# Two attention layers with a flagged fallback: the opening stage's work dealt anew over three engines, its value products moved earlier, and the first scores placed ahead of the flag's read

## The chip, the cores and the metric

The kernel runs on one core of a Trainium2 chip. The metric is the time of one execution on the device in microseconds (us); the kernel before took 882.53 us in the median of three runs. The engines of a core run their own instruction streams in order and wait for one another through semaphores: TensorE (PE) does matrix products, ScalarE (ACT) activations, VectorE (DVE) and GpSimd (POOL) elementwise work, SyncE (SP) issues the transfers.

## The reference, cut to what matters

```python
x = L0_attn_x                                   # (4, 1024, 128)
xn = _layernorm(x)
s = _L0_attn_ref(xn, ...)                       # its own layernorm of xn, qkv, 16 heads of 8, softmax, output product
g = _silu(_L0_ffn_ref(xn, W_fc, W_proj))        # relu squared FFN, then 5 spiking steps
x = x + s * g
xn = _layernorm(x)
s = _L1_attn_ref(xn, ...)                       # causal attention with position slopes
g = _silu(_L1_ffn_ref(xn, ...))                 # coupling network, 3 cycles
return x + s * g
```

Only what leads up to the first attention is touched: the double normalization of x, the products q, k and v of it, and the transposes of the two FFN weights.

## The kernel before

The 4096 tokens lie in 32 tiles of 128 tokens. The program has four stages on every engine: the prologue (`prologue`), the first attention (`first_attention`), a middle, the second attention. Each stage is a function that gives one part for each engine, and the parts are concatenated, so an engine goes from its prologue to its attention part without a barrier.

The prologue works in eight halves m = 0 to 7 of 512 tokens (four tiles each, the list `M`). For each half there are these steps:

- the normalized tiles `hs` (named xn in the trace), four tensor_scalar instructions in `normalized_by`, L337. VectorE does halves 0, 2 and 4, GpSimd 1, 3, 5, 6 and 7 (`ON_POOL`). They wait for the roots of the variances, which VectorE finds for tiles 0 to 7, 8 to 15 and 16 to 31 in three rounds; each ends in `rooted`.
- `turn(m)`: four transposes on TensorE, L575, into the PSUM bank `tr[m % 2]`; ScalarE copies them to `y`, L411 (`h_kept`).
- q and k: two products of 128x512 on TensorE, L604, into `pq[m % 2]`, which is free when the low parts of half m - 2 are done.
- each of q and k is kept as a high and a low part: ScalarE writes the high part (`high_of`, L414) and the square (`square_of`, L417), VectorE the low part (`low_of`, L490). SyncE stores both to DRAM, from where the stacked operands q_st and k_st are loaded.
- `norms_of(m)`: TensorE sums the squares by head, L585, into the bank `pn`; VectorE takes the maximum of each pair of halves (`peak_of`, L495).

Behind the last half TensorE does the v products of batch 0 (L612), the last norms, the transposes of the two FFN weights (L618, L621; ScalarE copies them, L455), and a transpose of the maxima (L624). VectorE turns them into `flag` in five small steps, L550 to L554: it says whether the scores could overflow. Then it does the last low parts and adds the bias to v (L563).

`row_maxima` follows: TensorE, VectorE and SyncE each read the flag into a register (TENSOR_LOAD, L671 on TensorE) and branch. With this input the flag is 0 and the body is skipped. Only then comes the first score of `first_attention`, L1165.

The first attention has 256 steps t. A step is four score products (L1165) into two of three PSUM slots, two exponentials of 128x1024 on ScalarE (L959), and the products with v (L1182) two steps later. Step t is work of pair t // 2; `side_fills` says at which pair a piece of other work is put between the steps on TensorE (`piece_of`) and on VectorE (`evacuate`). The first of these pieces is fc at pair 5.

Of the kernel before, what the change touches and what calls it, by code (L numbers as in the profile page):

```python
# [32 lines left out]
G = 4  # L33
# [252 lines left out]
def prologue(nc, a, s, x_t, room):  # L286
# [18 lines left out]
    norms, top, peak = piece(1, B), piece(1, 1), piece(1, P)[0:1, :]  # L305
# [19 lines left out]
    link, hs_rdy, hs_pool, tr_ps, ht_in, oned = (sem(x) for x in ("link", "hs_rdy", "hs_pool", "tr_ps", "ht_in", "oned"))  # L325
    qk_ps, kept, squared, lo_rdy, norm_ps, norm_in = (sem(x) for x in ("qk_ps", "kept", "squared", "lo_rdy", "norm_ps", "norm_in"))
    beta_ps, bv_rdy, ffn_ps, ffn_kept, v_ps = (sem(x) for x in ("beta_ps", "bv_rdy", "ffn_ps", "ffn_kept", "v_ps"))
    tail, peak_turned, v_kept = sem("tail"), sem("peak_turned"), sem("v_kept")
    stored = [s[f"stored0{m}"] for m in range(M)]
    room["first_flagged"], room["lows_done"], room["v_kept"] = tail, (lo_rdy, 2 * M), (v_kept, 2)  # L330

    def h_t(m):
        return s["y"][:, HT * m:HT * m + HT, :].rearrange("p t c -> p (t c)")

# [73 lines left out]
    def act_part(act):  # L408
        def h_kept(m):
            act.wait_ge(tr_ps, m + 1)  # L410
            nc.scalar.copy(h_t(m), tr[m % 2]).then_inc(ht_in, 1)  # L411

        def high_of(m, z):
            nc.scalar.activation(parts[m][:, z, 0, :], pq[m % 2][z], ACT.Identity, bias=b_col[:, z:z + 1]).then_inc(kept, 1)  # L414

        def square_of(m, z):
            nc.scalar.activation(square[m % 2][:, z, :], pq[m % 2][z], ACT.Square, bias=b_col[:, z:z + 1]).then_inc(squared, 1)  # L417

# [18 lines left out]
        for m in range(M):  # L437
            if m >= 2:
                act.wait_ge(norm_ps, m - 1)
            if m == M - 1:  # L440
                for z in range(2):
                    act.wait_ge(qk_ps, 2 * m + z + 1)
                    square_of(m, z)
                for z in range(2):
                    high_of(m, z)
                continue
            for z in range(2):
                if z == 1 and 2 <= m + 1 < M:
                    h_kept(m + 1)
                act.wait_ge(qk_ps, 2 * m + z + 1)  # L450
                high_of(m, z)
                square_of(m, z)
        for n, kept_t in enumerate((s["fc_t"], s["proj_t"])):
            act.wait_ge(ffn_ps, n + 1)
            nc.scalar.copy(kept_t[:, :, :], pq[0][n].rearrange("p (n f) -> p n f", n=FC)).then_inc(ffn_kept, 1)  # L455

    def dve_part(dve):
# [22 lines left out]
        def rooted_of(n0, n1):  # L480

            ch.after(nc.vector.tensor_scalar_mul(s["skip_r"][:, n0:n1], rstd[:, 1, n0:n1], GATE_SCALE))
            dve.sem_inc(rooted, 1)

        def normalized(m):
            normalized_by(nc.vector, m).then_inc(hs_rdy, 1)

        def low_of(m, z):
            dve.wait_ge(kept if m == M - 1 else squared, 2 * m + z + 1)
            nc.vector.scalar_tensor_tensor(parts[m][:, z, 1, :], pq[m % 2][z], b_col[:, z:z + 1],  # L490
                                           parts[m][:, z, 0, :].bitcast(F32), ALU.add, ALU.subtract).then_inc(lo_rdy, 1)

# [28 lines left out]
        normalized(2)  # L521
# [4 lines left out]
        for k in range(ROOT_STEPS):  # L526
            root(MIDDLE, NT, k)
            if k in (3, 6):
# [3 lines left out]
        normalized(4)  # L532
# [4 lines left out]
                                ALU.add).then_inc(bv_rdy, 1)  # L537
        ch.after(nc.vector.tensor_tensor(s["rho"][:, :], rstd[:, 1, :], rstd[:, 1, :], ALU.mult))
        nc.vector.tensor_tensor(s["rho"][:, :], s["rho"][:, :], var[:, 0, :], ALU.mult)
        for m in range(2, M - 1):  # L540
            low_of(m, 0)
            low_of(m, 1)
            if m % 2 == 0 and m > 2:
                peak_of(m // 2 - 1)
# [5 lines left out]
        tops.after(nc.vector.tensor_copy(peak, tr[0][0:1, 0:P]))  # L550
# [4 lines left out]
        low_of(M - 1, 0)  # L555
        low_of(M - 1, 1)
        dve.wait_ge(v_zero, 1)
        dve.wait_ge(v_preset, 1)
# [1670 lines left out]
```

## Time and profile before

| | us |
|---|---|
| median of three runs (880.74 to 882.54) | 882.53 |
| the profiled execution | 881.24 |
| its span, from the first to the last instruction | 879.4 |
| start of the first exponential of the attention | 52.62 |

1.84 us of the profiled execution lie outside the span. The page gives the busy time of each engine and, in 40 slices of 22 us, their busy share in tenths; the chain of waits says which instruction released the next; the timeline gives the instructions of an engine in order of time. The granted clock is the share of TensorE's full clock of 2.4 GHz: 1.00, or 0.50 for 1.2 GHz.

### The profile page before, as it was taken

What the parts mean: (1) busy time and instruction counts of PE and PEld (TensorE: products, weight loads), DVE (VectorE), ACT (ScalarE), POOL (GpSimd) and SP (SyncE); (2) the same over time, 40 slices, a digit from 0 to 9 for tenths busy, and PEclk for the clock granted to TensorE, in tenths of its full rate; (3) what the DMA queues carried; (4) which work ended last, traced back from release to release, by engine and by line L of the source; (5) the groups of instructions that cost most, each with busy time, mean ns of one, the idle gap of its engine ahead of it and who ended that gap; (6) DMA issues with size and microseconds to landing.
All of it is one profiled execution on the core that took longest, in us unless ns stands there. A gap on an engine that the chain in (4) does not pass through costs nothing.

```text
span 879.4 us, 21895 instructions
## 1 busy us (share of the span) xinstructions
PE 786.2 (89%) x9238; PEld 302.1 (34%) x9238; DVE 419.0 (48%) x884; ACT 827.2 (94%) x921; POOL 225.6 (26%) x272
## 2 busy tenths in 40 slices
PE   4769999899999999999999999997988988978976
PEld 2322434234343434433343433222332323323322
DVE  7731275464657662677537588996021121131132
ACT  7769999999999999999999996769999999999996
POOL 5401120121212041111303021203234334334333
PEclk9969999999999999999999999997999999999999
DMA  7892020110210300203000016100202113022000
GB/s 189 288 285 49 2 78 2 39 40 2 78 46 6 126 2 14 90 25 111 16 3 25 26 44 207 42 25 1 70 9 89 40 52 89 15 75 90 13 1 25
DMA packets 31947, 53.42 MB, mean 61 GB/s; under 512 B 5481, under 2 KB 16361, under 8 KB 31849
## 3 DMA queue, kind: packets, MB, share of 16 engines
q1 hardware_dynamic: 31848, 52.01, 18.8%
q8 instruction: 74, 1.21, 0.6%
q14 instruction: 25, 0.20, 0.1%
HBM read 31.29 MB, written 20.71 MB: 59 GB/s over the span
## 4 chain that ended last, share of the span: by engine, by line
PE 71%; ACT 18%; DVE 7%; issue 4%; DMA 0%; SPq 0%; DVEq 0%; ACTq 0%
PE c_ps L1182 27%; PE c_ps L1165 13%; ACT c_ring L1874 12%; PE c_ps L112 10%; PE c_ps L2027 8%; PE c_ps L2066 8%; ACT c_ring L959 3%; PE c_ps L1592 1%; DVE early L1537 1%; DVE c_th L463 1%; PE c_ps L1607 1%; ACT xs L1881 1%; PE c_ps L1599 1%; ACT c_ring L1395 1%; DVE y L1540 1%
## 5 line engine op out<-in xcount | busy, mean ns | idle before, releaser
L959 ACT ACTIVATE c_ring<-c_ps 128x1024 f32<-128x1024 f32 x512 | 473.7, 1032 | 7.3 <-PE c_ps L1165 7.0
L1182 PE MATMUL c_ps<-c_ring,vt 128*18 128x256 f32 (+1 forms) x3072 | 272.3, 457 | 0.0
L1874 ACT ACTIVATE c_ring<-c_ps 128x1024 f32<-128x1024 f32 x288 | 267.9, 1070 | 2.4 <-PE c_ps L2027 2.0
L2066 PE MATMUL c_ps<-c_ring,vt 128*18 128x384 f32 (+3 forms) x1672 | 152.7, 467 | 2.4 <-issue 0.9
L1165 PE MATMUL c_ps<-q_st,k_st 32*128 32x512 f32 x1024 | 131.4, 501 | 25.5 <-ACT c_ring L959 20.5
L1899 POOL TENSOR_SCALAR_AFFINE_SELECT c_ring<-c_ring 128x512 f32<-128x512 f32 x128 | 84.3, 677 | 182.3 <-ACT c_ring L1874 182.3
L1182 PEld LDWEIGHTS c_ps<-c_ring,vt 128*18 128x18 f32 x3072 | 64.9, 97 | 143.0 <-issue 103.1
L2027 PE MATMUL c_ps<-q_st,k_st 32*128 32x512 f32 (+3 forms) x768 | 80.0, 418 | 35.1 <-ACT c_ring L1874 31.9
L1165 PEld LDWEIGHTS c_ps<-q_st,k_st 32*128 32x128 f32 x1024 | 50.5, 183 | 142.1 <-ACT c_ring L959 132.8
L980 POOL TENSOR_TENSOR early<-early 128x512 f32<-128x512 f32 x32 | 38.4, 1201 | 176.3 <-DVE early L1103 176.3
L2027 PEld LDWEIGHTS c_ps<-q_st,k_st 32*128 32x128 f32 x768 | 39.8, 186 | 106.3 <-ACT c_ring L1874 94.4
L2066 PEld LDWEIGHTS c_ps<-c_ring,vt 128*18 128x18 f32 x1672 | 35.3, 97 | 58.8 <-issue 43.6
L1933 DVE STREAM_TRANSPOSE ext<-c_ps 128x512 f32<-128x512 f32 x15 | 10.8, 717 | 93.5 <-PE c_ps L2066 93.5
L1103 DVE TENSOR_SCALAR early<-c_ps 128x512 f32<-128x512 f32 x32 | 22.1, 690 | 63.5 <-PE c_ps L112 63.5
L1107 DVE TENSOR_SCALAR y<-c_ps,rho 128x128 f32<-128x128 f32 x32 | 9.0, 344 | 83.4 <-PE c_ps L112 83.4
L966 POOL TENSOR_TENSOR early<-early,y 128x512 f32<-128x512 f32 x7 | 10.6, 1512 | 142.6 <-DVE early L1118 142.6
L1395 ACT ACTIVATE c_ring<-c_ps,cn_b 128x512 f32<-128x512 f32 (+1 forms) x30 | 25.1, 858 | 16.5 <-PE c_ps L1592 9.6
L988 POOL TENSOR_TENSOR c_th<-parts 128x512 bf16<-128x512 f32 x12 | 15.4, 1287 | 82.7 <-DVE parts L1135 82.7
L112 PE MATMUL c_ps<-proj_t,early 128*32 128x128 f32 x1024 | 33.8, 273 | 0.0
L112 PE MATMUL c_ps<-y,fc_t 128*32 128x512 f32 x256 | 33.3, 592 | 0.0
L1954 DVE COPY y<-c_ps 128x512 f32<-128x512 f32 x8 | 5.5, 692 | 58.0 <-PE c_ps L2079 58.0
L112 PEld LDWEIGHTS c_ps<-proj_t,early 128*32 128x32 f32 x1024 | 29.3, 110 | 5.9
(242 smaller groups left out, 774.3 us busy)
## 6 DMA issues: line engine op xcount, KB each, us to landing
q_st<-q_hl SPq DMA_DIRECT2D x48, 256.0 KB
k_st<-k_hl SPq DMA_DIRECT2D x48, 256.0 KB
q_hl<-parts SPq DMA_DIRECT2D x10, 512.0 KB, 4.1
k_hl<-parts SPq DMA_DIRECT2D x10, 512.0 KB, 4.3
q_hl<-c_ring SPq DMA_DIRECT2D x4, 512.0 KB, 3.8
k_hl<-c_ring SPq DMA_DIRECT2D x4, 512.0 KB, 4.6
out_dram<-x SPq DMA_DIRECT2D x7, 256.0 KB, 3.7
x<-in_L_attn_x_dram SPq DMA_DIRECT2D x3, 512.0 KB, 5.8
```

Of the source, the lines that this page charges most:

```text
L112: ins = nc.tensor.matmul(out[c:c + COLUMN, :], weight[:, c:c + COLUMN], rows, start=start, stop=stop, tile_position=(0, c))
L959: nc.scalar.activation(probs[t % RING][:, 2 * pair:2 * pair + 2, :], scores[unit % SLOTS][:, :, :], ACT.Exp).then_inc(expd, 1)
L980: pool.tensor_tensor(hidden[f], hidden[f], hidden[f], ALU.mult).then_inc(hid_rdy, 1)
L988: pool.tensor_tensor(square[hf][:, z, :], high, high, ALU.mult).then_inc(sq_rdy, 1)
L1103: ins = nc.vector.tensor_scalar_max(hidden[hf[1]], side[:, :], 0.0)
L1165: ins = nc.tensor.matmul(scores[(2 * t + i // 2) % SLOTS][:, i % 2, :], k_st[part, g, kt * P:(kt + 1) * P], q_st[part, g, qh * HALF:(qh + ...
L1182: ins = nc.tensor.matmul(o_ps[32 * h:32 * h + 2 * W9, c0:c1], vt[b % 2][:, kt, gp, h, W9 * gs:W9 * gs + 2 * W9], probs[t % RING][:, h, c0: ...
L1395: nc.scalar.activation(out, source, ACT.Gelu, bias=bias[:, 0:1]).then_inc(squashed[z], 1)
L1874: nc.scalar.activation(probs[t % RING][:, first:first + 2, :], scores[unit % SLOTS][:, :, :], ACT.Exp).then_inc(expd, 1)
L1899: ins = pool.affine_select(out=part, in_=part, compare_op=ALU.is_ge, fill=0.0, base=0, pattern=[[0, G], [1, P]], channel_multiplier=-1)
L2027: ins = nc.tensor.matmul(banks[i][:, at:at + w], k_st[part, 2 * gp + gs, kt * P:(kt + 1) * P], q_st[part, 2 * gp + gs, qh * HALF + q0:qh * ...
L2066: ins = nc.tensor.matmul(o_ps[32 * h:32 * h + 2 * W9, q0:q0 + w], vt[b % 2][:, kt, gp, h, W9 * gs:W9 * gs + 2 * W9], probs[t % RING][:, h, ...
```

## The change

- Halves: ScalarE normalizes halves 2 and 4 (`ON_ACT`, four activations each, with a new tile `shift` of minus mean times root, which VectorE makes in each of the three rounds), VectorE 0 and 6, GpSimd 1, 3, 5 and 7.
- From half 4 on (`SHARED`) the high part of k is VectorE's (`high_of` in its part) and no longer ScalarE's; ScalarE's last half takes its squares first.
- The transposes have one PSUM bank `tr` instead of two, the other banks are dealt anew, so that the two slots of the first scores hold nothing that is late.
- On TensorE, turn(m + 1) stands behind the products of half m for m = 1 to 4 and ahead of them for m = 5 and 6. The v products are cut in two: four behind the norms of half 1, four behind those of half 3. VectorE's additions move along.
- The transposes of the FFN weights leave the prologue: they are two new pieces "turn" at pairs 2 and 3 of the attention, evacuated by VectorE and no more by ScalarE.
- The four score products of step 0 stand behind the transpose of the maxima and ahead of the flag's read (`first_ahead`). Behind the read, step 0 only waits for them and posts two counts of `scored`. In the flagged body they are done again.

ScalarE in the prologue before, halves 1 and 2. The names: y takes the transposed half, c_ring the high part (parts of the ring buffer), on the squares, xn the normalized tiles.

```order
L414 ACTIVATE c_ring<-c_ps,b_col 128x512 [waits p_qk_ps]
L417 ACTIVATE on<-c_ps,b_col 128x512
L411 COPY y<-c_ps 128x512 [waits p_tr_ps]
L414 ACTIVATE c_ring<-c_ps,b_col 128x512 [waits p_qk_ps]
L417 ACTIVATE on<-c_ps,b_col 128x512
L414 ACTIVATE c_ring<-c_ps,b_col 128x512 [waits p_qk_ps,p_norm_ps]
```

The same place after:

```order
L421 ACTIVATE c_ring<-c_ps,b_col 128x512 [waits p_qk_ps]
L427 ACTIVATE on<-c_ps,b_col 128x512 [waits p_qk_ps]
L432 ACTIVATE xn<-x,c_th 128x128 [waits p_rooted]
L432 ACTIVATE xn<-x,c_th 128x128 x3
L417 COPY y<-c_ps 128x512 [waits p_tr_ps]
L421 ACTIVATE c_ring<-c_ps,b_col 128x512 [waits p_qk_ps]
```

The copy of half 2 stood between the two parts of half 1; it now stands behind all four of its activations and behind four more that make the tiles it copies.

TensorE at the end of the prologue before, from the last q and k products to the first score's branch:

```order
L604 MATMUL c_ps<-y,w 128x512
L585 MATMUL c_ps<-on,head_of 32x512 [waits p_norm_in,p_squared]
L585 MATMUL c_ps<-on,head_of 32x512
L612 MATMUL c_ps<-w,y 128x128 [waits p_bv_rdy]
L612 MATMUL c_ps<-w,y 128x128 x7
L585 MATMUL c_ps<-on,head_of 32x512 [waits p_squared]
L585 MATMUL c_ps<-on,head_of 32x512
L618 MATMUL c_ps<-ident,gathered 128x128 [waits p_ffn_in,p_lo_rdy]
L618 MATMUL c_ps<-ident,gathered 128x128 x3
L621 MATMUL c_ps<-ident,gathered 128x128 x4
L624 MATMUL c_ps<-ident,c_th 1x128 [waits p_tail]
L671 TENSOR_LOAD flag [waits p_tail,p_ffn_kept]
```

And after:

```order
L626 MATMUL c_ps<-y,w 128x512
L640 MATMUL c_ps<-on,head_of 32x512 [waits p_norm_in,p_squared]
L640 MATMUL c_ps<-on,head_of 32x512
L640 MATMUL c_ps<-on,head_of 32x512 [waits p_squared]
L640 MATMUL c_ps<-on,head_of 32x512
L669 MATMUL c_ps<-ident,c_th 1x128 [waits p_v_kept,p_tail]
L1208 MATMUL c_ps<-q_st,k_st 128x512 [waits p_lo_rdy,p_v_kept,staged00]
L1208 MATMUL c_ps<-q_st,k_st 128x512 x3
L717 TENSOR_LOAD flag [waits p_tail]
```

The v products and the weights' transposes are gone from here, and four score products stand ahead of the read.

The core of the diff:

```diff
-    ON_POOL = (1, 3, 5, 6, 7)
+    ON_POOL, ON_ACT, ON_DVE = (1, 3, 5, 7), (2, 4), (0, 6)
+    SHARED = 4
...
-    tr = [lower[:, 0, :], upper[:, 2, :]]
-    pn, misc = lower[:, 1, :], upper[:, 3, :]
+    tr, early_v = lower[:, 0, :], lower[:, 1, :]
+    pn, misc = upper[:, 2, :], upper[:, 3, :]
...
+        def normalized(m):
+            act.wait_ge(rooted, (1, 2, 3, 3)[m // 2])
+            for n in range(HT * m, HT * m + HT):
+                ins = nc.scalar.activation(hs[:, n, :], s["x"][:, n, :], ACT.Identity, bias=shift[:, n:n + 1],
+                                           scale=rstd[:, 0, n:n + 1])
+            ins.then_inc(hs_act, 1)
...
         for m in range(M):
+            if m >= SHARED:
+                if m > SHARED and m + 1 < M:
+                    h_kept(m + 1)
+                if m < M - 1:
+                    high_of(m, 0)
+                square_of(m, 0)
+                square_of(m, 1)
+                if m == M - 1:
+                    high_of(m, 0)
+                if m == SHARED:
+                    h_kept(m + 1)
                 continue
             for z in range(2):
                 high_of(m, z)
                 square_of(m, z)
+            if m >= 1:
+                if m + 1 in ON_ACT:
+                    normalized(m + 1)
+                h_kept(m + 1)
...
         for m in range(M):
+            if m > SHARED and m + 1 < M:
+                turn(m + 1)
+            qk_of(m)
+            if 1 <= m <= SHARED:
                 turn(m + 1)
             if m >= 1:
                 norms_of(m - 1)
+            if m == 2:
+                v_of(0, early_v)
+            if m == SHARED:
+                pe.wait_ge(bv_rdy, 1)
+                v_of(1, misc)
         norms_of(M - 1)
         pe.wait_ge(tail, 1)
+        pe.wait_ge(v_kept, 2)
+        nc.tensor.matmul(misc[0:1, 0:P], top, s["ident"][:, :], start=True, stop=True).then_inc(peak_turned, 1)
...
+        if b == 0:
+            fill("turn", 0, 0, 2)
+            fill("turn", 0, 1, 3)
...
+    def first_ahead(pe):
+        pe.wait_ge(staged[0], 16 * LOADS)
+        pe.wait_ge(*room["early_v_read"])
+        pe.wait_ge(*room["lows_done"][0])
+        first_scores(pe)
...
+            if t == 0:
+                pe.wait_ge(ahead, 2)
+                pe.sem_inc(scored, 2)
+                return
...
             for unit in (2 * t, 2 * t + 1):
                 if unit >= SLOTS:
                     pe.wait_ge(expd, unit - SLOTS + 1)
-                elif unit == SLOTS - 1:
-                    pe.wait_ge(*room["lows_done"])
+                elif unit >= 1:
+                    pe.wait_ge(*room["lows_done"][unit - 1])
...
                 begin_pe(pe)
+                room["first_ahead"](pe)
                 bound_pe(pe)
                 first_pe(pe)
```

## Rows read from the trace of the kernel before

**Rows 1.** Groups of ScalarE from 66.4 us on: busy, mean ns, idle before
```profile
L959 ACT ACTIVATE c_ring<-c_ps 128x1024 f32<-128x1024 f32 x500 | 462.1, 1032 | 0.8 <-PE c_ps L1165 0.7
```
**Rows 2.** Stretches: length, busy PE, PEld, DVE, ACT, POOL, granted clock, DMA
```profile
0.00:52.60 52.60, 29.84 (x116) 15.73 (x116) 37.60 (x160) 35.55 (x49) 22.27 (x47) 0.98 0.80 246
52.60:66.40 13.80, 9.80 (x68) 2.93 (x72) 1.98 (x9) 11.70 (x13) 0.00 (x0) 0.56 0.85 282
```
**Rows 3.** Chain of waits up to 80 us: start, us, what
```profile
31.70 1.11 PE c_ps L604 x2
32.89 0.69 ACT early L414
33.58 0.58 ACT on L417
34.16 0.56 ACT y L411
...
48.88 2.85 issue
```
**Rows 4.** Timeline of ScalarE, prologue and first steps: start, us
```profile
12.65 0.40 ACT L433 ACTIVATE w<-c_th 128x128 f32<-128x128 f32 x1
12.95 0.50 ACT L434 ACTIVATE w<-c_th 128x256 f32<-128x256 f32 x1
...
19.12 0.70 ACT L417 ACTIVATE on<-c_ps,b_col 128x512 bf16<-128x512 f32 x1
20.64 0.59 ACT L411 COPY y<-c_ps 128x512 f32<-128x512 f32 x1 [0.83 <-PE c_ps L575]
...
52.62 1.94 ACT L959 ACTIVATE c_ring<-c_ps 128x1024 f32<-128x1024 f32 x2 [4.62 <-PE c_ps L1165]
...
61.67 1.94 ACT L959 ACTIVATE c_ring<-c_ps 128x1024 f32<-128x1024 f32 x2 [0.64 <-PE c_ps L1165]
...
66.33 13.87 ACT L959 ACTIVATE c_ring<-c_ps 128x1024 f32<-128x1024 f32 x15 [0.16 <-PE c_ps L1165]
```
**Rows 5.** Timeline of VectorE in the prologue
```profile
18.77 1.12 DVE L337 TENSOR_SCALAR xn<-x,mean,c_th 128x128 f32<-128x128 f32 x4
...
46.34 0.69 DVE L495 TENSOR_REDUCE c_th<-c_ps 128x1 f32<-128x512 f32 x1 [2.89 <-PE c_ps L585]
...
48.72 0.14 DVE L554 TENSOR_SCALAR flag<-c_th 1x1 int32<-1x1 f32 x1
```
**Rows 6.** Timeline of TensorE in the prologue and at the first steps
```profile
11.05 1.08 PE L575 MATMUL c_ps<-ident,xn 128*128 128x128 f32 x4 [11.05 <-DVE xn L337]
...
19.94 0.66 PE L575 MATMUL c_ps<-ident,xn 128*128 128x128 f32 x4 [0.87 <-DVE xn L337]
...
22.41 1.96 PE L604 MATMUL c_ps<-y,w 128*128 128x512 f32 x4 [1.48 <-issue]
...
40.95 1.98 PE L604 MATMUL c_ps<-y,w 128*128 128x512 f32 x4 [0.35 <-ACT y L411]
...
43.92 2.05 PE L612 MATMUL c_ps<-w,y 128*128 128x128 f32 x16
...
47.28 0.38 PE L624 MATMUL c_ps<-ident,c_th 128*1 128x128 f32 x2
...
63.35 0.80 PE L1165 MATMUL c_ps<-q_st,k_st 32*128 32x512 f32 x4
...
67.50 0.51 PE L1165 MATMUL c_ps<-q_st,k_st 32*128 32x512 f32 x4 [0.70 <-ACT c_ring L959]
```
**Rows 7.** The flag's read on TensorE: duration min/median/max, first and last start
```profile
L671 PEldq TENSOR_LOAD <-flag x2: 314/1182/2049, 49.0 to 594.8; - x2
```
**Rows 8.** TensorE by quarter us: length, busy, granted clock, DMA share, GB/s
```profile
51.00:51.25 0.25, 0.00 (x0) 0.50 0.91 147
...
64.50:64.75 0.25, 0.25 (x4) 0.73 0.95 262
```
**Rows 9.** The q and k products: duration min/median/max, first and last start
```profile
L604 PE MATMUL c_ps<-y,w x32: 592/592/1061, 14.1 to 42.3; 128*128 128x512 f32 x32
```

More of the change, by code:

```diff
@@ L485, in normalized, with high_of, v_of @@
         def normalized(m):
[L486 removed]
+            normalized_by(nc.vector, m).then_inc(hs_dve, 1)
+        def high_of(m):
+            dve.wait_ge(squared, 2 * m + 2)
+            nc.vector.tensor_scalar(parts[m][:, 1, 0, :], pq[m % 2][1], b_col[:, 1:2], None, ALU.add).then_inc(hi_rdy, 1)
         def low_of(m, z):
[L489 removed]
+            if z == 1 and m >= SHARED:
+                dve.wait_ge(hi_rdy, m - SHARED + 1)
+            elif m == M - 1:
+                dve.wait_ge(kept, kept_count(m, z))
+            else:
+                dve.wait_ge(squared, 2 * m + z + 1)
             nc.vector.scalar_tensor_tensor(parts[m][:, z, 1, :], pq[m % 2][z], b_col[:, z:z + 1],
                                            parts[m][:, z, 0, :].bitcast(F32), ALU.add, ALU.subtract).then_inc(lo_rdy, 1)
+        def v_of(hf, bank):
+            if hf == 0:
+                dve.wait_ge(v_zero, 1)
+                dve.wait_ge(v_preset, 1)
+            dve.wait_ge(v_ps, hf + 1)
+            for s2 in range(2):
+                dst, src, add = v_columns(bank, s["vt"][0], s["bv0"], hf, s2)
+                ins = nc.vector.tensor_tensor(dst, src, add, ALU.add)
+            ins.then_inc(v_kept, 1)
         def peak_of(b):
@@ L1150, in dve_part, with first_scores, first_again @@
             extra(2 * pair // PER, pair % (PER // 2))
+    def first_scores(pe):
+        for i in range(G):
+            part = slice(STACK * i, STACK * i + STACK)
+            ins = nc.tensor.matmul(scores[i // 2][:, i % 2, :], k_st[part, 0, 0:P], q_st[part, 0, 0:HALF], start=True, stop=True)
+            if i % 2 == 1:
+                ins.then_inc(ahead, 1)
+    def first_ahead(pe):
[3 more added lines that the diff above has]
+        first_scores(pe)
+    def first_again(pe):
+        first_scores(pe)
+        pe.wait_ge(ahead, 4)
     def pe_part(pe):
         def score(t):
+            if t == 0:
+                pe.wait_ge(ahead, 2)
+                pe.sem_inc(scored, 2)
+                return
             b, gp, qh, gs, kt = place(t)
@@ L1191, in piece_of @@
                 ins = by_columns(nc, side[:, :], s["fc_t"][:, hf[1], :], flat("y", b, hf[0]))
+            elif kind == "turn":
+                fc, proj = room["ffn_raw"]
+                pe.wait_ge(*room["ffn_in"])
+                for f in range(FC):
+                    ins = nc.tensor.transpose(side_tiles[:, f, :], proj[:, f * P:(f + 1) * P] if hf else fc[:, f, :],
+                                              s["ident"][:, :])
             elif kind == "y":
```

119 lines of the change are left out of this document (57 added, 62 removed).

## The prediction, made before the changed kernel was run

> **What bounds the kernel now.** I read the groups of instructions first. From 66.4 us on, ScalarE runs 500 exponentials of the first attention with 0.8 us of idle time before them in all [rows 1]. Nothing that the change touches lies there or in the stages behind, so those keep their length, and the change is worth what it moves the point from which ScalarE runs without pauses, 66.33 us [rows 4]. Ahead of that point the view by stretches shows two parts. In the prologue, up to 52.60 us, every engine has slack by its sum (VectorE 37.60 us busy, ScalarE 35.55, TensorE 29.84), so waits between engines set the time. From 52.60 to 66.40 us ScalarE is 11.70 of 13.80 us busy and TensorE's mean clock is 0.56 [rows 2]. The chain of waits names the loop in the prologue: product, high part, square, copy of the next half, product, each step waiting for the one before; 31.70, 32.89, 33.58, 34.16, and the next product at 34.76. It also names the gap at the end: 2.85 us of issue between the flag and the first score [rows 3], of which the flag's read on TensorE is 2.05 us [rows 7]. The clock record says that TensorE went to half its clock (1.2 GHz) at 51.0 us, when it had done nothing since its last transpose ended at 47.66 [rows 6] but wait for the flag, and came back to 2.4 GHz at 64.6 us, after six us of almost unbroken work [rows 8].
>
> **Halves 2 and 4 on ScalarE.** Before, VectorE makes half 2 in 1.12 us from 18.77 [rows 5], beside ScalarE, which is busy with half 1; the copy of half 2 starts at 20.64 [rows 4]. After, ScalarE makes it itself, behind its four activations of half 1. The last of the three that it had done by then starts at 19.12; a high part and a square of 0.58 and 0.65 us more (the spacing in the chain, 32.89 to 33.58 to 34.16, and its neighbours) free it at about 20.95. The nearest row for the new instruction is the one 128x128 activation, 0.40 us long, with the next one 0.30 us behind [rows 4]: three spacings and one length make 1.3 us, so the tiles are there at 22.3. The transposes (0.66 us [rows 6]) are done at 23.0, the copy at 23.6, and the products of half 2 start at 23.7 against 22.41 before [rows 6]: +1.3 us. VectorE, relieved of 1.03 us, has the low parts of half 0 ready at about 21.4; they set the start before, and are no longer late. Half 3 keeps the distance (+1.3). Half 4 goes the same way once more: ScalarE ends half 3 at about 31.6, the tiles are there at 32.9, the copy at 34.15, and the products start at 34.2 against 31.70 [rows 3]: +2.5 us. The bounds for one half: with a spacing of 0.22 us it is 1.06 us instead of 1.3, with one of 0.40 (no overlap at all) 1.6. Over both halves that is -0.5 to +0.6 us.
>
> The Trainium skill (ScalarE: Activation LUTs, section Rules for kernel authors) budgets about 0.3 us for an activation plus 0.83 ns for each element, 0.41 us for one of 128, and 0.85 us more than I take over both halves. The trace has 0.40 us as the length of one such instruction and 0.30 us as its spacing, from a single pair.
>
> **Halves 4 to 7 with the shared work.** Between half 4 and half 5 TensorE has 1.8 us of products, 0.55 of transposes, 0.35 of norms and now half of the v products, 1.0 us (half of 2.05 [rows 6]): 3.7 us, and behind them the transposes of half 6, which stand ahead of the products of half 5 and must find the one bank empty. So half 5 starts at 38.5, 3.7 us late. Now the cuts pay. With the copies ahead of the high parts and one activation less on ScalarE, the loop of 3.1 us (31.70 to 34.76 [rows 3]) is open: TensorE's own work, 2.7 us, sets the pace, and half 6 starts at 41.2. Half 7 has no transposes in front and starts at about 43.4, where it waits for the low part of half 5, the last of three VectorE instructions of 0.65 to 0.75 us; 2.4 us late against 40.95 [rows 6].
>
> **The end of the prologue.** Before, the maximum at 46.34 waits 2.89 us for the norms [rows 5], and those stand behind the v products [rows 6]. After, the squares come first and the v products are gone: the squares of half 7 end at 46.1, the norms at 46.5, the maximum starts at 46.6. VectorE is free by then only just (its low parts of half 6 end at about 46.6). So 2.1 us are won back of 2.4, and the flag is written at 49.1 instead of 48.86 [rows 5]: +0.2 us. A second pass with 0.05 us added to every handover gives +0.8; I take **+0.5**, with bounds of 0 and +1.1 from the activation's spacing.
>
> **The first scores ahead of the read.** Before, the score starts 2.85 us behind the flag and the exponential 0.90 us later, at 52.62 [rows 3, 4]. After, the four products lie ahead of the read, hidden behind VectorE's five steps to the flag, and the count is posted when the branch is through. The exponential starts some 2.7 us behind the flag: **-1.05 us**. That holds if the read still takes 2.05 us. Step 1 needs the low parts of half 7, now three VectorE instructions behind the flag, done 2.2 us after it and so in time for 52.8.
>
> **The weights' transposes as pieces.** ScalarE's copies of them cost nothing before, since it was idle until 52.62. On TensorE eight transposes now lie in pairs 2 and 3, the first four ahead of the score of step 5, at 63.35 us, when the clock is low and TensorE is what ScalarE waits for, 0.64 us before step 4 already [rows 4]. Four such transposes take 1.08 us at the low clock [rows 6], 0.9 apart, and there is no cover. The four in pair 3 come at the high clock, 0.6 us, into a pause of 0.70 us [rows 6]. **+0.9 us**, with bounds of 0 (clock high in both) and +1.8 (low in both).
>
> **The sum.** +0.5 - 1.05 + 0.9 = +0.35 us on the profiled execution, 881.24 us, of which the span is 879.4. That run lies 1.3 us under the median of the three, which themselves span 1.8 us. The changed kernel's median is then about 882.53 + 0.3, and I say **882.8 us**. A measurement of this kernel tells changes of over 0.2%, 1.8 us, from none; this one is inside.
>
> **The rivals.** *TensorE loses its clock in the new pauses (slower).* Behind the products of half 1 TensorE now stands still from 19.1 to 22.3 us, and behind those of half 3 from 29.8 to 32.9, 3.2 us each, where it had 0.87 and then 1.48 us [rows 6]. The fall at 51.0 came 3.4 us after its last work [rows 8]. If it falls in one, the products of the next half or two run at 1061 ns a record instead of 592 [rows 9]: the first product lands 0.85 us later, the transposes take 0.4 us more, and the flag moves by 1.3 us for one half to 2.1 for two. With the sum that is 884.1 to 884.9. Against it: both pauses are a bit shorter than the one that led to a fall. It decides if the activations are dearer than 1.3 us a half and the pauses so grow towards that one. Chance 0.22, half of it beyond 0.2%.
>
> *The clock stays or comes up early in the first steps (faster).* At 2.4 GHz nothing holds the exponentials: 12 of them at the steady spacing of 0.925 us (13.87 us for 15 [rows 4]) take 11.1 us and not the 13.7 from 52.62 to 66.33. That is 2.6 us, and the 0.9 of the pieces goes too: 882.8 - 3.5 = 879.3. Against it: TensorE still pauses, from 48.5 to 52.9 us, 4.4 us. For it: with the pieces its work from 58 us on is denser, which could end the low stretch some us earlier and give a part, 880.5. Chance 0.14.
>
> *The flag's read is short.* The second read of the program takes 0.31 us [rows 7], at a time when hardly a transfer runs; the first has transfers at their full rate around it. If the stores are thinner at 49 us, 1.7 us go: 881.1. Chance 0.12; it leaves the sign at "same" unless the front of the prologue is also cheap.
>
> The Trainium skill (DMA: Bandwidth & Descriptors, section Latency and other measured facts) gives about 0.6 us as the floor of such a load; by it the read would give back up to 1.45 us, and the sum would be 881.4. The trace has one read under that floor and one at three times it, so the floor decides nothing here.
>
> *The prologue costs what the sum says or a little more*, by the spacing of the activations: the forecast, 881.6 to 884, chance 0.52.
>
> **How the numbers follow.** Slower by over 0.2%, beyond 884.3: half of the first rival, 0.11, and the upper edge of the forecast with both dear pieces, 0.10: 0.21. Faster by over 0.2%, under 880.8: most of the second rival, 0.12, a part of the third with a cheap front, 0.05, and 0.04 for cuts in the shared halves that I priced too low: 0.21. Same: 0.58. The range of 879.9 to 884.9 leaves out the full gain of the clock and a second fall of it.
>
> **What would show each step.** In the changed profile: products of half 2 at about 23.7 us, half 4 at 34.2, half 7 at 43.4 (front); the four new activations 0.3 us apart; the last maximum at 46.6 with under 0.3 us of wait; the flag at 49.1 to 49.7; no score product between the read and the first exponential, which starts at 51.8 to 52.4; a low clock from 51 us or earlier until 61 to 65; ScalarE idle before step 5 for 1.5 us and no more pauses from about 66.7 us on. The prediction is wrong if the products of half 4 start before 33 us, if the read is under 1 us, or if the granted clock drops before 45 us.

## The result, and the profile after

The changed kernel took **884.41 us** in the median of 20 runs (882.15 to 886.71), the kernel before 882.25 us in the 20 beside them (880.74 to 882.82). The ratio is 1.003, with a 95% interval of 1.0024 to 1.0036: slower by 0.3%. The time lies in the forecast's range, but of its cases the first rival came true, the clock that falls in the new pauses, and not the likeliest one, no change. One execution in all the runs of this document, of e9_peak_read, took 1751 us, twice as long as the others, and is left out of that kernel's median and ratio. The profiled execution took 884.42 us with a span of 882.7, against 881.24 and 879.4 before.

The page of the changed kernel shows where to look first: the granted clock of TensorE in the second of the 40 slices is 0.8, and the busy share of TensorE in the first two slices is 3 and 7.

```profile
PE   3769999899999999999999999997988988978976
...
PEclk9869999999999999999999999997999999999998
```

The same two stretches as [rows 2] by length, busy time of PE, PEld, DVE, ACT and POOL, granted clock and DMA:

```profile
0.00:52.60 52.60, 31.61 (x108) 15.88 (x108) 37.80 (x160) 35.07 (x51) 18.98 (x43) 0.93 0.77 245
52.60:66.40 13.80, 8.25 (x52) 2.98 (x56) 2.96 (x7) 9.69 (x10) 0.00 (x0) 0.53 0.87 279
```

Up to 52.60 us the mean clock is 0.93 instead of 0.98, and TensorE is busy 1.8 us longer with fewer instructions. Up to 66.40 us 10 exponentials are done where 13 had been started before.

The timeline of TensorE in the prologue (start, us, idle time before and what ended it), with L617 the transposes and L626 the products of q and k:

```profile
23.06 0.66 PE L617 MATMUL c_ps<-ident,xn 128*128 128x128 f32 x4 [3.42 <-ACT xn L432]
...
24.40 3.55 PE L626 MATMUL c_ps<-y,w 128*128 128x512 f32 x4 [0.35 <-ACT y L417]
...
34.93 1.11 PE L617 MATMUL c_ps<-ident,xn 128*128 128x128 f32 x4 [3.17 <-ACT xn L432]
...
36.72 2.76 PE L626 MATMUL c_ps<-y,w 128*128 128x512 f32 x4
...
41.60 1.88 PE L626 MATMUL c_ps<-y,w 128*128 128x512 f32 x4
...
44.23 1.88 PE L626 MATMUL c_ps<-y,w 128*128 128x512 f32 x4
...
46.37 1.98 PE L626 MATMUL c_ps<-y,w 128*128 128x512 f32 x4
```

Two pauses, 3.42 and 3.17 us long, end with ScalarE's tiles (`xn L432`). Right behind each, the granted clock is at half (1.2 GHz): length, busy, clock, DMA of two stretches.

```profile
25.00:27.00 2.00, 2.00 (x4) 0.50 0.60 226
...
35.00:37.00 2.00, 1.86 (x7) 0.50 0.86 318
```

The products of half 2 start at 24.40 against 22.41 [rows 6], half 4 at 36.72 against 31.70 [rows 3], half 7 at 46.37 against 40.95 [rows 6]. The end of the chain on VectorE, TensorE's read of the flag, and ScalarE at the first steps:

```profile
51.95 0.14 DVE L601 TENSOR_SCALAR flag<-c_th 1x1 int32<-1x1 f32 x1
```

```profile
L717 PEldq TENSOR_LOAD <-flag x2: 313/925/1537, 52.1 to 597.0; - x2
```

```profile
54.47 8.11 ACT L1010 ACTIVATE c_ring<-c_ps 128x1024 f32<-128x1024 f32 x8 [4.82 <-PEq L1226]
63.22 1.94 ACT L1010 ACTIVATE c_ring<-c_ps 128x1024 f32<-128x1024 f32 x2 [0.64 <-PE c_ps L1239]
66.42 19.42 ACT L1010 ACTIVATE c_ring<-c_ps 128x1024 f32<-128x1024 f32 x21 [1.27 <-PE c_ps L1239]
```

The flag is 3.2 us late (51.95 against 48.72 [rows 5]), the first exponential 1.85 (54.47 against 52.62 [rows 4]). A good mark for the whole is the thirteenth exponential, from which ScalarE ran without pauses before, at 66.33 us [rows 4]. Here the eleventh starts at 66.42, and two spacings of 0.925 us later, at 68.27, the thirteenth: 1.9 us late. That is most of the 2.2 us between the medians. The profiled execution is longer by more, 3.2 us. By its timelines the distance to before is 2.2 us at the first exponential of the second attention (600.17 against 597.93), and 2.8 us a few steps later, where TensorE's clock comes back later (between 611 and 614 us, before between 606 and 609) and ScalarE has a second pause, of 0.64 us. The last four products add 0.5 us (1.22 against 0.71). No edit lies in these places.

### The profile page after: what moved, and what is told of

Same layout as the page of the kernel before. It is cut to its first block, busy times and chain, and to the rows that moved or that the text cites. A ratio compares the mean times of both kernels' runs of the same rounds, so it can differ in the third digit from the quotient of the medians.

```text
span 882.7 us, 21909 instructions
## 1 busy us (share of the span) xinstructions
PE 790.3 (90%) x9238; PEld 303.9 (34%) x9238; DVE 422.7 (48%) x889; ACT 826.6 (94%) x923; POOL 222.4 (25%) x268
## 4 chain that ended last, share of the span: by engine, by line
PE 73%; ACT 18%; DVE 5%; issue 3%; DMA 0%; PEldq 0%; SPq 0%; DVEq 0%; ACTq 0%
PE c_ps L1256 27%; PE c_ps L1239 13%; ACT c_ring L1955 12%; PE c_ps L112 10%; PE c_ps L2147 8%; PE c_ps L2108 8%; ACT c_ring L1010 3%; PE c_ps L626 2%; PE c_ps L1673 1%; DVE early L1618 1%; PE c_ps L1688 1%; PE c_ps L617 1%; ACT xs L1962 1%; PE c_ps L1680 1%; ACT c_ring L1476 1%
```

## The experiments

In the table "13th" is the start of the thirteenth exponential in the profiled execution, worked out as above, and the ratio is to the kernel before, measured beside each group: its median was 881.70 us beside e1 to e4, 882.09 beside b1 and e6 to e8, and 880.92 beside e9 to e11. Flag, first exponential and 13th come from one profiled execution each.

| kernel | flag | first exp. | 13th | median us | ratio, 95% interval |
|---|---|---|---|---|---|
| before | 48.72 | 52.62 | 66.33 | 882.25 | 1 |
| changed | 51.95 | 54.47 | 68.27 | 884.41 | 1.0030 (1.0024 to 1.0036) |
| e1_dve_halves | 48.63 | 51.91 | 65.72 | 881.78 | 0.9987 (0.9974 to 1.0001) |
| e2_read_first | 52.04 | 55.51 | 68.89 | 884.74 | 1.0028 (1.0016 to 1.0040) |
| e3_pieces_later | 53.03 | 55.47 | 67.92 | 884.20 | 1.0022 (1.0013 to 1.0032) |
| e4_busy_pauses | 50.69 | 53.25 | 66.19 | 882.11 | 1.0005 (0.9996 to 1.0013) |
| b1_act_halves | 54.51 | 57.35 | 69.80 | 884.69 | 1.0032 (1.0020 to 1.0044) |
| e6_peak_early | 45.81 | 47.65 | 61.68 | 877.45 | 0.9953 (0.9939 to 0.9966) |
| e7_peak_late | 46.74 | 48.83 | 62.30 | 877.99 | 0.9952 (0.9939 to 0.9966) |
| e8_busy_more | 48.98 | 51.63 | 64.37 | 881.26 | 0.9991 (0.9981 to 1.0001) |
| e9_peak_read | 45.83 | 48.86 | 61.87 | 877.48 | 0.9959 (0.9946 to 0.9972) |
| e10_peak_again | 45.88 | 47.74 | 61.61 | 877.42 | 0.9958 (0.9945 to 0.9971) |
| e11_after_peak | 52.93 | 55.42 | 69.24 | 884.17 | 1.0033 (1.0020 to 1.0046) |

### Halves 2 and 4 back on VectorE

```diff
-    ON_POOL, ON_ACT, ON_DVE = (1, 3, 5, 7), (2, 4), (0, 6)
+    ON_POOL, ON_ACT, ON_DVE = (1, 3, 5, 7), (), (0, 2, 4, 6)
...
         rooted_of(EARLY, MIDDLE)
+        normalized(2)
...
         rooted_of(MIDDLE, NT)
+        normalized(4)
         low_of(2, 0)
```

> The changed kernel with one part undone: halves 2 and 4 are normalized by VectorE again, as before. Theory A (the four activations at 0.42 us each behind ScalarE's other work, and TensorE's fall to half its clock in the two pauses that they open, are what made the kernel slower): the products of half 2 start at 22.5 us instead of 24.4, those of half 4 at 31 to 32 instead of 36.7, no clock below 1.00 before 50 us, the flag at about 48 us instead of 52.1, and the time is 3 to 4 us under the changed kernel, about 881 us, 1 us or more under the kernel before. Theory B (the single transpose bank and the v products in between are what cost): half 7 still starts after 43 us, the flag comes after 50 us, and the time stays within 1 us of the changed kernel's 884.4.

The loss is gone (ratio 0.9987), and so are the two pauses for ScalarE. But TensorE found another wait, ahead of the products of half 4, and the clock fell before 50 us all the same, against what Theory A said. Its timeline in this kernel, L628 being the products and L642 the norms:

```profile
29.37 0.66 PE L619 MATMUL c_ps<-ident,xn 128*128 128x128 f32 x4 [0.34 <-DVE xn L343]
32.41 0.61 PE L642 MATMUL c_ps<-on,head_of 128*32 128x512 bf16 x2 [2.38 <-DVE c_th L534]
32.95 3.22 PE L628 MATMUL c_ps<-y,w 128*128 128x512 f32 x4
```

The norms of half 2 wait 2.38 us for VectorE's first maximum (L534), and the products behind them run at the low clock again, 3.22 us for four. VectorE's timeline says why the maximum was late; it stands behind the low parts of half 2 and the whole of half 6 (`xn L343`, the second one):

```profile
28.20 1.11 DVE L343 TENSOR_SCALAR xn<-x,mean,c_th 128x128 f32<-128x128 f32 x4 [0.15 <-DVE skip_r L502]
29.23 1.41 DVE L519 SCALAR_TENSOR_TENSOR c_ring<-c_ps,b_col,c_ring 128x512 fp32r<-128x512 f32 x2
30.55 1.18 DVE L343 TENSOR_SCALAR xn<-x,mean,c_th 128x128 f32<-128x128 f32 x4
31.57 0.69 DVE L534 TENSOR_REDUCE c_th<-c_ps 128x1 f32<-128x512 f32 x1
```

The single times of this kernel fall in two groups, four runs at 878.2 to 878.4 us and eight at 881.1 to 882.6; only one of the second group has a trace here. Over the whole execution the granted clock is 0.987 in each run of the first group and 0.982 to 0.984 in the second. That the first group is runs in which the clock did not fall in this wait fits these figures but is not shown.

### The scores behind the read again

```diff
...
                 begin_pe(pe)
-                room["first_ahead"](pe)
                 bound_pe(pe)
+                room["first_ahead"](pe)
```

> The changed kernel with the four first scores behind the flag's read instead of ahead of it (the step for a raised flag, which this input does not run, is left as it was before). Theory A: the exponential starts 3.3 us or more behind the flag instead of 2.4, the time is 0.9 us above the changed kernel, 885.3. Theory B (the read takes what is left of some other wait, so where the scores stand does not matter): the first exponential keeps its distance of 2.4 us and the time is the same within 0.3 us.

The first exponential comes 3.33 us behind the flag (52.18 to 55.51) instead of 2.38: the scores ahead are worth 1.0 us there. At the thirteenth exponential 0.6 us of it is left (68.89 against 68.27). In the ratios it can't be seen, 1.0028 against 1.0030, but the interval of the first is 1 us wide to either side. The same pair was run once more in a better kernel, below.

### The weight pieces one pair later

```diff
-            fill("turn", 0, 0, 2)
-            fill("turn", 0, 1, 3)
+            fill("turn", 0, 0, 3)
+            fill("turn", 0, 1, 4)
```

> The changed kernel with the two transposed weight pieces at pairs 3 and 4 of the attention instead of 2 and 3. Theory A (at pair 2 the clock is low and TensorE sets the pace): ScalarE's pause of 1.27 us before step 5 shrinks to some 0.5 us, the time is 0.6 to 0.9 us under the changed kernel. Theory B (the piece adds work that brings the clock back earlier, so that it pays for itself): the low stretch lasts longer and the time is the same within 0.3 us.

The pause of 1.27 us ahead of the eleventh exponential is gone in the profile. The ratio of 1.0022 overlaps with the changed kernel's 1.0030, so this run does not tell whether the pieces cost nothing or 1 us and more; nor does e7_peak_late, below.

### Idle transposes in the two pauses

```diff
         def turn(m):
+            if m >= 1:
+                pe.wait_ge(ht_in, m)
+            if m in ON_ACT:
+                for k in range(16):
+                    nc.tensor.transpose(tr[:, 0:P], s["ident"][:, :], s["ident"][:, :])
             if m in ON_POOL:
...
-            if m >= 1:
-                pe.wait_ge(ht_in, m)
             for t in range(HT):
```

> The changed kernel with 16 idle transposes of the unit matrix on TensorE in each of the two pauses, ahead of the transposes of halves 2 and 4 (about 2 us of work that nobody reads). Theory A (the pauses cost twice: by their length, and by the clock that falls in them): the clock stays at 1.00 up to 50 us, the four products of half 2 take 1.98 us instead of 3.55 and those of half 4 1.98 instead of 2.76, the flag comes 2 to 3 us earlier, and the time is 1.5 to 3 us under the changed kernel with the activations as they are. Theory B (TensorE isn't what the chain waits for there): the flag moves by less than 0.5 us.

These transposes compute nothing that is used; they only keep TensorE at work while ScalarE makes its tiles. They bring back 2.2 us by the two ratios (1.0030 to 1.0005). The flag comes 1.3 us earlier, not the 2 to 3 of Theory A. The timeline of TensorE: 16 transposes (L612) in each pause, and behind them the rest of it.

```profile
19.70 1.91 PE L612 MATMUL c_ps<-ident 128*128 128x128 f32 x16
23.16 0.66 PE L620 MATMUL c_ps<-ident,xn 128*128 128x128 f32 x4 [1.56 <-ACT xn L432]
...
24.50 3.31 PE L629 MATMUL c_ps<-y,w 128*128 128x512 f32 x4 [0.35 <-ACT y L417]
...
36.24 1.99 PE L629 MATMUL c_ps<-y,w 128*128 128x512 f32 x4 [0.35 <-ACT y L417]
```

In the second pause the clock stayed, and the products of half 4 take 1.99 us; in the first it still fell, 3.31 us. Hence the next run.

### The same with 26 of them

```diff
-                for k in range(16):
+                for k in range(26):
```

> The changed kernel with 26 idle transposes in each of the two pauses of TensorE's instead of 16, so that the pauses (3.42 and 3.17 us) are filled nearly to their end. Theory A (the clock falls in these pauses and is the larger part of the loss): the products of half 2 now run at the full clock too (about 2.0 us for the four instead of 3.3), half 7 and the flag come 0.7 to 1.4 us earlier than with 16 (flag at about 49.5 to 50), the whole 0.5 to 1.2 us shorter than with 16: ratio to before 0.999 to 1.000. Theory B (what 16 of them won was in another place, the length of the pauses is the loss): the time within 0.3 us of the kernel with 16, ratio 1.0005, or longer, if the idle transposes run into the half's own.

Now the clock holds in both places:

```profile
18.65 3.00 PE L612 MATMUL c_ps<-ident 128*128 128x128 f32 x26
22.61 0.66 PE L620 MATMUL c_ps<-ident,xn 128*128 128x128 f32 x4 [0.95 <-ACT xn L432]
...
23.94 1.98 PE L629 MATMUL c_ps<-y,w 128*128 128x512 f32 x4 [0.35 <-ACT y L417]
...
34.54 1.98 PE L629 MATMUL c_ps<-y,w 128*128 128x512 f32 x4 [0.35 <-ACT y L417]
```

The flag comes at 48.98 instead of 51.95, and the ratio is 0.9991. Halves 2 and 4 are still ScalarE's, and TensorE still does its own work only when their tiles are there; what differs is the clock. By the two ratios (1.0030 to 0.9991) the clock in the two pauses is worth 0.39% of the time, more than 3 us and more than the whole loss, and all the rest of the change, the length of the pauses included, comes to about -0.8 us, which the interval (0.9981 to 1.0001) can't tell from nothing.

### One part alone: the kernel before with halves 2 and 4 on ScalarE

```diff
-    ON_POOL = (1, 3, 5, 6, 7)
+    ON_POOL, ON_ACT, ON_DVE = (1, 3, 5, 6, 7), (2, 4), (0,)
...
+        def normalized(m):
+            act.wait_ge(rooted, (1, 2, 3, 3)[m // 2])
+            for n in range(HT * m, HT * m + HT):
+                ins = nc.scalar.activation(hs[:, n, :], s["x"][:, n, :], ACT.Identity, bias=shift[:, n:n + 1],
+                                           scale=rstd[:, 0, n:n + 1])
+            ins.then_inc(hs_act, 1)
```

> The kernel before with one part of the change alone: halves 2 and 4 are normalized by ScalarE (four activations of 128x128 each), nothing else is dealt anew. Theory A (the two halves on ScalarE at 0.417 us for each activation open two pauses of TensorE, in which its clock falls, and this is the loss): products of half 2 from 22.4 to about 24.4, those of half 4 from 31.7 to about 36, both at the granted clock 0.50; the flag at 51.5 to 53 where before it was at 48.7, and the whole 3 to 4 us longer than before, ratio about 1.004. Theory B (the loss comes out of the other shares, the sums of squares and remainders of the late halves): the late halves are as before here, the flag within 0.7 us of before, the ratio 0.999 to 1.001.

This part alone makes the kernel before slower by 0.32%, as much as the whole change. Its TensorE has the same two pauses and the same low clock behind them:

```profile
22.53 1.02 PE L588 MATMUL c_ps<-ident,xn 128*128 128x128 f32 x4 [3.83 <-ACT xn L423]
...
24.23 2.90 PE L617 MATMUL c_ps<-y,w 128*128 128x512 f32 x4
...
33.45 1.11 PE L588 MATMUL c_ps<-ident,xn 128*128 128x128 f32 x4 [3.23 <-ACT xn L423]
...
35.24 3.78 PE L617 MATMUL c_ps<-y,w 128*128 128x512 f32 x4
```

Its flag is even later (54.51) than expected (51.5 to 53): the products of half 4 start at 35.24, 1.5 us before those of the changed kernel, but take 3.78 us. Behind them the old loop of 3.1 us a half [rows 3] and the v products ahead of the last norms remain: half 7 starts at 46.74, and from there to the written flag it is 7.9 us, as before, where the changed kernel needs 5.7. In these two profiles the rest of the change pays 2.6 us at the flag and 1.5 at the thirteenth exponential; the ratios, 1.0032 and 1.0030, do not show it.

### Halves 2 and 4 on VectorE, the first maximum early

```diff
         rooted_of(MIDDLE, NT)
+        normalized(4)
+        peak_of(0)
         low_of(2, 0)
         low_of(2, 1)
         normalized(6)
-        peak_of(0)
```

> The changed kernel with halves 2 and 4 back on VectorE as in the run before this one, and with VectorE's first maximum of norms (for which TensorE waited 2.38 us there, ahead of the products of half 4) put right behind half 4's normalization instead of behind half 6's. Theory A (the head is bounded by what TensorE waits for, one wait after another): products of half 4 at about 31.2 instead of 32.95 and at the full clock, the flag at about 46.5 to 47.2 instead of 48.6, and the whole 1 to 2 us below the kernel before (880 to 881, ratio about 0.998). Theory B (behind that wait the late halves are bound by GpSimd's four halves and by ScalarE): products of half 4 earlier, but half 7's and the flag within 0.4 us of the run without this edit, ratio 0.9985 to 1.0.

This beats both kernels: 877.45 us, a ratio of 0.9953. The same kernel was measured again, unchanged:

> The kernel with halves 2 and 4 on VectorE and the first maximum put early, once more, beside the other two of this call, and to see whether its gain comes again: Theory A (the gain is the head's, with a flag at about 45.8 instead of 48.7): 877.4 to 878.4, ratio to before 0.995 to 0.996. Theory B (a lucky series of runs, the first kernel with the halves on VectorE had four runs at 878.3 as well): 879 to 881.

877.42 us, 0.9958, as its Theory A said. The gain, about 4 us, is larger than either theory of the first run said. Ahead of the products of half 4 TensorE now waits 0.88 us, the clock stays up in all eight halves (it falls at 45.3 us, in the wait for the flag), and they run through:

```profile
22.89 1.96 PE L628 MATMUL c_ps<-y,w 128*128 128x512 f32 x4 [1.48 <-ACT y L417]
...
31.34 1.96 PE L628 MATMUL c_ps<-y,w 128*128 128x512 f32 x4 [0.88 <-DVE c_ring L519]
...
35.41 1.88 PE L628 MATMUL c_ps<-y,w 128*128 128x512 f32 x4
...
40.23 1.98 PE L628 MATMUL c_ps<-y,w 128*128 128x512 f32 x4
```

Half 4 comes 1.6 us earlier than in e1_dve_halves (31.34 against 32.95) and its four products are 1.3 us shorter: 2.9 us at half 5, and 2.8 at the flag. Against e8_busy_more, where the clock holds too, half 4 comes 3.2 us earlier (31.34 against 34.54) and so does the flag (45.81 against 48.98): with the clock up in both, this is what the two pauses cost by their length. (The idle transposes and the place of the first maximum differ as well.) The flag's read was also short in this kernel:

```profile
L719 PEldq TENSOR_LOAD <-flag x2: 311/590/869, 46.0 to 590.3; - x2
```

### The first maximum early, in the changed kernel

```diff
         rooted_of(MIDDLE, NT)
+        peak_of(0)
         low_of(2, 0)
         low_of(2, 1)
         normalized(6)
-        peak_of(0)
```

> The changed kernel with only the first maximum of norms put ahead of VectorE's remainders of half 2; halves 2 and 4 stay on ScalarE. Theory A (TensorE waits there for ScalarE's half 4 until 34.9 us, so that the maximum has no one who waits for it): flag and time as in the changed kernel, 884 to 885, ratio 1.002 to 1.003. Theory B (the early maximum by itself is what gained 4 us in the other kernel): 880 to 882.

Nothing, 1.0033. Where TensorE waits for ScalarE's tiles, nobody waits for the maximum. The 4 us are of the two edits together. In this profile both pauses are 3.17 us long, under the 3.2 that the prediction reckoned with, and the four transposes behind them take 1.1 us, as they do at half the clock. This is the second:

```profile
35.92 1.11 PE L617 MATMUL c_ps<-ident,xn 128*128 128x128 f32 x4 [3.17 <-ACT xn L432]
```

### The pieces later, in the good kernel

> The same kernel with the first weight pieces put at pairs 3 and 4 as well instead of pairs 2 and 3. Theory A (a piece in the pause ahead of the fourth pair comes at the low clock and holds scores back): about 0.6 us less than the kernel without this, ratio to it 0.9993. Theory B (the total there is set by ScalarE's exponentials from about 60 us on, and the scores catch up): the same to within 0.2 us.

The edit is that of e3_pieces_later, on e6_peak_early. The ratio is 0.9952 against 0.9953: no difference can be seen. With five runs of each and an interval of over 1 us to either side this does not rule out Theory A's 0.6 us. Nor do the two profiles: from the first to the thirteenth exponential it is 13.5 us here and 14.0 in e6_peak_early, 0.6 us less, but in this execution the clock fell ahead of half 2 (its lines are in the last section), which made the flag 0.9 us late.

### The scores behind the read, in the good kernel

> The kernel with halves 2 and 4 on VectorE and the first maximum put early, with one thing undone: the first scores stand behind the flag's read again. Theory A (the first exponential comes 1.0 us earlier by the scores ahead, and in a head without the two pauses this is kept): first exponential about 2.8 us behind the flag instead of 1.8, the whole 0.8 to 1.1 us longer than the kernel without this, ratio between the two about 1.001. Theory B (the read has the same end whatever stands beside it, and what is won at the first exponential is lost again at the fourth pair, as the same edit undid nothing in the changed kernel itself): the two times within 0.3 us of each other.

The edit is that of e2_read_first. The two kernels, run side by side, took 877.48 (five runs) and 877.42 us (five runs), within the 0.3 us of Theory B, though runs of one kernel differ by up to 1.8 us. Yet the first exponential is 1.1 us later, as foretold. Here is ScalarE in the kernel with the scores behind the read,

```profile
48.86 1.94 ACT L1008 ACTIVATE c_ring<-c_ps 128x1024 f32<-128x1024 f32 x2 [5.32 <-PEq L1224]
...
60.02 12.96 ACT L1008 ACTIVATE c_ring<-c_ps 128x1024 f32<-128x1024 f32 x14 [0.17 <-PE c_ps L1237]
```

and in the one with the scores ahead (e10_peak_again):

```profile
47.74 1.94 ACT L1012 ACTIVATE c_ring<-c_ps 128x1024 f32<-128x1024 f32 x2 [4.14 <-PEq L1228]
...
59.76 12.96 ACT L1012 ACTIVATE c_ring<-c_ps 128x1024 f32<-128x1024 f32 x14 [1.03 <-PE c_ps L1241]
```

Of 1.1 us at the first exponential 0.26 are left at the eleventh. TensorE's clock tells where the rest went: it came back at 58.0 us with the scores behind the read, and at about 58.7 with the scores ahead. It had also fallen earlier with the scores behind, at about 47.8 us, and at 48.5 with the scores ahead. First the one, then the other (length, busy, clock, DMA share, GB/s):

```profile
46.00:48.00 2.00, 0.16 (x4) 0.94 1.04 391
...
58.00:58.50 0.50, 0.50 (x12) 1.00 1.05 406
```

```profile
48.00:50.00 2.00, 0.80 (x4) 0.62 1.07 271
...
58.00:58.50 0.50, 0.50 (x9) 0.50 1.02 385
58.50:59.00 0.50, 0.50 (x8) 0.78 1.04 389
```

So the low stretch was as long in both, about 10.2 us, and lay 0.7 us later with the scores ahead; at its end TensorE sets the pace and ScalarE pauses (1.03 us ahead of the eleventh exponential). What sets the two moments was not found out. It isn't the code alone: in e6_peak_early, the same kernel as e10_peak_again, the clock fell at 45.3 and came back at 58.9 us.

## Why the prediction was right or wrong, point by point

**The bound.** Right: all that the change was worth shows in the start of the unbroken exponentials. It moved by 1.9 us and the medians by 2.2. The profiled execution is longer by 3.2 us; its rest arose behind 66 us, where no edit lies.

**The activations.** Too cheap, and the front's figures with them. I took three spacings of 0.30 and one length of 0.40 us from the activation of [rows 4]; four of the new ones take 1.66 and 1.65 us instead of 1.3. All instances of that line, with minimum, median and maximum duration:

```profile
L432 ACT ACTIVATE xn<-x,c_th x8: 491/507/523, 21.3 to 34.4; 128x128 f32<-128x128 f32 x8
```

One is 0.51 us long and the spacing is (1.65 - 0.51) / 3 = 0.38. The row I priced by was the same size but not the same form: L433 takes one column operand, the scale, and L432 two, scale and bias. The Trainium skill (ScalarE: Activation LUTs, section What ACT_TABLE_LOAD costs) says that each such operand adds about 93 ns; the two rows differ by 0.11 us. The 0.41 us of the rule that the prediction weighed and left aside was nearer: four of them are 1.64 us a half. That is 0.7 us over both halves more than the prediction took, and not the 0.85 written there. What they cost the path was less, as the next point shows. Over both halves 0.7 us is also just outside the bounds that the prediction gave, -0.5 to +0.6.

**The clock in the pauses.** This is the step that failed: the forecast held TensorE at its full clock through the two new pauses, by the argument that they were shorter than the one of 3.4 us behind which it had fallen before [rows 8]. The clock fell behind both pauses (3.42 and 3.17 us), and so before 45 us, which the prediction itself had named as a sign of being wrong. It had this fall as its first rival, with the right mechanism, but with the wrong condition: the activations were dearer, yet the second pause did not grow over 3.2 us, nor did either of the two in e11_after_peak (3.17 us each), and the clock fell all the same. The old pause had only told that 3.4 us are enough, and nothing on less. The rival's price, 2.1 us at the flag for two halves, was a little low. With the clock held, in e8_busy_more, the flag comes 3.0 us earlier (51.95 to 48.98), of which 0.46 lies ahead of the pauses' end, at the products of half 2 (24.40 and 23.94): 2.5 us are left. The half's transposes and products and a part of the next half's run at half speed, and ScalarE and VectorE then wait for them. The products of half 4 came at 36.72, not 34.2. In e8_busy_more, with the same activations, they come at 34.54, 0.3 us from the forecast; so 2.2 of the 2.5 us are not the activations' but the clock's and the 0.46. Its chance of 0.22 rested on the argument from the pauses' length.

**The shared halves.** Right in their pace where the clock was full: 2.63 us from half 5 to 6 and 2.14 to half 7 (2.7 and 2.2 foretold), 5.7 us from the last products to the flag (5.7 foretold, 7.9 before [rows 5, 6]). Between half 4 and 5 lie 4.9 us instead of 4.3; in e8_busy_more, with the clock up, it is 4.1 us.

**The flag.** 3.2 us late where I took +0.5 with an upper bound of +1.1: the bounds held the spread of the activations but not the rival. A step whose rival is that likely needs a range over both.

**The scores ahead of the read.** Right in place and size at the first exponential: it starts 2.4 us behind the flag (2.7 foretold), 1.0 us earlier than with the scores behind the read. The read took 1.54 us, not 2.05. Too much in the sum: of the 1.0 and 1.1 us in the two pairs 0.6 and 0.26 are left at the thirteenth exponential. The medians of both pairs show none; together they speak against the full 1.05 us, but cannot tell a part of it from nothing. I had carried a gain at the start of a stretch through to its end, while part of the stretch hangs on something else, the moment at which the clock comes back.

**The weight pieces.** The first pause grew from 0.64 to 1.27 us, as foretold in kind (1.5 us were named), and there is none in the next pair. From the first to the thirteenth exponential it is 13.80 us instead of 13.71, so of the +0.9 us only 0.1 shows there. What the pieces cost by themselves stays open: with them one pair later no difference can be seen in the better kernel (0.9952 against 0.9953), but 0.9 us lies within the interval.

**The sum.** +0.35 us was foretold and +2.2 came. In the profiles the three terms are +3.2 at the flag (+0.5 foretold), -1.4 from the flag to the first exponential (-1.05; 0.5 of it is the shorter read) and +0.1 from there to the thirteenth (+0.9), together 1.9. That the time still lies in the range is partly luck. The upper end, 884.9 us, was meant to leave out a second fall of the clock, and the second fall came. With +3.2 at the flag and the other two terms as foretold the time would have been 882.25 + 3.05 = 885.3 us, outside.

**The other rivals.** The clock came back at 65.6 us, not early (64.6 before). The read was a little shorter, 1.54 us; it took from 0.87 to 2.30 us in the kernels here, and no run shows what sets it.

## What to carry to other kernels

Before moving work from one engine to a slower one, look at what TensorE does meanwhile: a pause that grows costs its own length and then the clock for several us behind it. In this kernel the two costs were about equal. With the clock held the ratio goes from 1.0030 to 0.9991, over 3 us, and without the pauses to 0.9953, some 3 us more. Idle matmuls in such a pause are a quick experiment that tells the two apart, and here they also made good the loss. When a wait is removed, look at what stands in front of the next thing waited for: moving one reduction of 0.69 us three places up took 0.34% off (0.9987 to 0.9953).

And a gain at the start of a stretch is only a gain if the end of that stretch moves with it; that needs a row at the end, here the thirteenth exponential. A difference of under 1 us between two kernels can't be read from five runs of each here.

## What the runs showed of the hardware that I had not expected

- TensorE's clock fell to half behind pauses of 3.17 to 3.83 us, and in e7_peak_late (its timeline below) also ahead of the products of half 2, where TensorE had been idle for 1.46 and 1.48 us with 0.9 us of work between them (3.58 us for the four products). In e6_peak_early the rows are 0.70 and 1.48 us, and it did not fall; the code up to there is the same. Between a pause that costs nothing and one that brings the clock down lies little room, and it isn't the same in each execution.

```profile
20.30 0.66 PE L619 MATMUL c_ps<-ident,xn 128*128 128x128 f32 x4 [1.46 <-DVE xn L343]
...
22.77 3.58 PE L628 MATMUL c_ps<-y,w 128*128 128x512 f32 x4 [1.48 <-issue]
```

- The length of the last pause alone does not tell when the clock falls. In the changed kernel it fell at 52.0 us, 0.7 us behind the end of the first scores (51.31), in e6_peak_early at 45.3, 0.1 us behind them (45.18), in both with waits of 0.98 us and 0.45 us shortly before; in e10_peak_again, the same kernel as e6_peak_early, only at 48.5 us.
- The same read of the flag took 2.05, 1.54, 2.30, 1.66, 1.17 and 0.87 us in six kernels (before, changed, e1_dve_halves, e8_busy_more, b1_act_halves, e6_peak_early), always with transfers running, and 0.31 us in each of them at its second place, some 540 us later. In e10_peak_again, the same kernel as e6_peak_early, it took 0.87 us too.
- The clock comes up for the first time at a moment that differs from execution to execution: the same first eight products of q and k took 5.38 us in the changed kernel and 4.53 in e8_busy_more, where the code up to there is the same. So a single profile can be 0.5 us off ahead of any edit (the products of half 2 start at 24.40 and 23.94).

```profile
14.26 5.38 PE L626 MATMUL c_ps<-y,w 128*128 128x512 f32 x8
```

```profile
14.29 4.53 PE L629 MATMUL c_ps<-y,w 128*128 128x512 f32 x8
```

- Starting the attention's steps 1.1 us earlier did not bring the clock back earlier (58.7 us in e10_peak_again, 58.0 in e9_peak_read, one execution of each).
